# Six banks for the score tiles and two for everything else, in the two attentions with heads of eight columns

## The reference, cut to what matters

```python
latent = x @ Wc_down
q = (latent @ Wq_up).reshape(B, T, 16, 8)
k, v = split(latent @ Wkv_up)              # one k and one v of 8 columns
att = softmax(where(causal, q k^T / sqrt(8), -inf))
x = x + (att @ v).reshape(B, T, 128) @ Wc_proj
```

## Time and profile before

| | us |
|---|---|
| median of three runs | 2706.16 (2706.14 to 2712.98) |
| span of the profiled execution | 2704.96, shown as 2705.0 |
| PE busy | 2422.2 (90%) |
| DVE, ACT, POOL busy | 1665.1, 1493.2, 1428.0 |
| exponentials of `Narrow` (line 1189) | 256, two stages of 128 |

### The profile page before, as it was taken

One profiled execution on the slowest core, in us unless ns is written; L12 is line 12 of the kernel. 1 busy time (PEld: TensorE's weight loads), 2 busy tenths in 40 slices (PEclk: granted clock), 3 DMA queues, 4 the chain that ended last, 5 costly groups with the idle time before them and its releaser, 6 DMA issues. The chain is left out here.

```text
span 2705.0 us, 62888 instructions
## 1 busy us (share of the span) xinstructions
PE 2422.2 (90%) x24633; PEld 1886.2 (70%) x24633; DVE 1665.1 (62%) x4392; ACT 1493.2 (55%) x3193; POOL 1428.0 (53%) x2261
## 2 busy tenths in 40 slices
PE   3999999999997688887999899999999877688887
PEld 3888888888885455556777777777777666455555
DVE  4677777777765567764544466666666522566656
ACT  3666666666653367774444455555555422466664
POOL 4778787787876644433333244444444412665544
PEclk9999999999998789998999999999999989799998
DMA  3691000000000100000000000000000054000000
GB/s 111 215 335 50 2 2 2 2 2 2 2 2 1 36 17 2 2 2 21 2 1 1 3 4 6 5 4 6 5 4 6 7 158 144 17 7 7 4 2 32
DMA packets 23255, 83.14 MB, mean 31 GB/s; under 512 B 4113, under 2 KB 11026, under 8 KB 21938
## 3 DMA queue, kind: packets, MB, share of 16 engines
q1 hardware_dynamic: 19810, 71.90, 8.1%
q0 software_dynamic: 3152, 7.21, 0.8%
HBM read 71.89 MB, written 46.79 MB: 44 GB/s over the span
## 5 line engine op out<-in xcount | busy, mean ns | idle before, releaser
L825 POOL TENSOR_TENSOR XR<-XR,T 128x256 f32<-128x256 f32 x512 | 375.7, 734 | 442.0 <-DVE T L708 411.9
L589 ACT ACTIVATE P<-ps 128x384 f32<-128x384 f32 (+1 forms) x512 | 250.6, 542 | 189.0 <-PE ps L2398 189.0
L2398 PE MATMUL ps<-P,V 128*64 128x256 f32 (+3 forms) x4096 | 332.7, 346 | 2.0 <-ACT P L589 2.0
L1189 ACT ACTIVATE P<-ps 128x768 f32<-128x768 f32 x256 | 207.9, 813 | 148.7 <-PE ps L2398 148.6
L1261 DVE TENSOR_REDUCE qa<-ps 128x2 fp32r<-128x512 f32 x256 | 176.7, 690 | 166.5 <-PE ps L2398 165.2
L2398 PEld LDWEIGHTS ps<-P,V 128*64 128x64 f32 (+1 forms) x4096 | 185.5, 123 | 100.9 <-issue 5.6
L2398 PE MATMUL ps<-mk,identb 128*128 128x256 bf16 (+1 forms) x1024 | 196.9, 295 | 58.9 <-DVE qa L1262 56.6
L719 DVE TENSOR_REDUCE sm<-ps 128x2 f32<-128x512 f32 (+1 forms) x256 | 130.6, 552 | 182.1 <-PE ps L2398 181.3
L1351 POOL TENSOR_SCALAR_AFFINE_SELECT P<-P 128x512 f32<-128x512 f32 x256 | 163.2, 638 | 136.6 <-ACT P L1189 136.2
L836 POOL TENSOR_TENSOR ss<-ss,nhalf 128x16 f32<-128x16 f32 x64 | 187.8, 2935 | 5.3
L2398 PE MATMUL ps<-QH,KH 64*128 64x256 f32 (+1 forms) x1024 | 165.6, 315 | 8.7 <-DVE QL L677 0.6
(11 more groups left out here) (320 smaller groups left out, 7285.5 us busy)
## 6 DMA issues: line engine op xcount, KB each, us to landing
rows_i<-in_zero SPq DMA_DIRECT2D x16, 1208.0 KB, 31.1
rows_o<-in_zero SPq DMA_DIRECT2D x16, 1208.0 KB, 79.6
w<-in_m_w SPq DMA_DIRECT2D x23, 578.0 KB, 4.0
zt<-rows_i SPq DMA_DIRECT2D x23, 128.0 KB, 3.1
rows_o<-yo POOLq DMA_DIRECT2D x23, 128.0 KB, 3.9
stg<-in_t_w SPq DMA_DIRECT2D x11, 256.0 KB, 2.6
XR<-in_x SPq DMA_DIRECT2D x4, 512.0 KB, 7.9
out<-XR SPq DMA_DIRECT2D x8, 256.0 KB, 2.0
```

Of the source, the lines that this page charges most:

```text
L589: e.activation(self.P[at % 6][:, :], K.ps.ap("st", s, g, h)[:, 0:self.w], ACT.Exp, bias=0.0, scale=1.0 if kind == 0 else 0.125).then_inc(K ...
L825: p = po.e.tensor_tensor(x, x, self.T[g % 2][:, par, pr], ALU.add)
L1189: e.activation(self.P[(2 * g + n) % 6][:, :, 0:384], K.ps.ap("st", s, g, n)[:, :, 0:384], ACT.Exp, bias=0.0, scale=self.scale).then_inc(K. ...
L2398: return self.te.matmul(o, l, r, start=start, stop=True, skip_group_check=True)
```

## The change

In class `Narrow` the ring of the scores gets a third pair (banks 4 and 5), which it takes from the ring of single banks. That one keeps banks 6 and 7.

```diff
-    SC, G = (8, 9), (4, 5, 6, 7)
+    SC, G = (8, 9, 10), (6, 7)
```

## The result

The changed kernel takes 2970.59 us (median of 4 runs, 2965.64 to 2972.59) against 2706.15 before: ratio 1.0964, 95% interval 1.0945 to 1.0984. It is slower by 264 us.

A forecast was written before the change was run, and what follows sets the result against it. PE, waiting for DVE's second maximum (line 1262), was taken to bound the kernel. With the lower clock, kind 1's +204 and kind 3's +130, together +332, on 2705.0 gave 3037, given as 3035; range 2850 to 3115 us.

The forecast's parts named there:

- What bounds the kernel: Steady kind 1: PE busiest, 88%, waiting most for DVE's second maximum, line 1262; a loop of about 1.98 us a half-step.
- the third pair: Score ring: masks go ahead of the wait for line 1262, loop 1.98 to 1.66 us; gain at most 77 us.
- Two single banks: Each take waits for the second last one's reader; at full clock +97 us in kind 1, +58 in kind 3.
- The low-clock sum of kind 3: One batch of eight half-steps in kind 3 with the clock at 1.2 GHz throughout: 33.35 us.
- pT's bank: DVE reads pT after both maxima, so takes bound to it start 1.52 us after an exponential's start; pv half-steps 3.14.
- The clock: PE's thin stretches lower it: kind 1 nine tenths low, +204 us; kind 3 half low, +130 us.
- The sum: Whole kernel: 2705.0 + 332 = 3037 us, given as 3035; +155 without the clock.
- Only kind 1 low: Rival: lower clock in kind 1 only, 202 + 58 us, time 2966; chance 0.16.
- The clock stays up: Rival: full clock in both stages, only the waits cost, 2706 + 155 = 2861 us; chance 0.20.
- The gain that was bounded at 77 us: Rival: faster, third pair counts, masks freed from the wait for line 1262, at most 77 us, 2629; chance 0.03.
- the case that I held the likeliest: Clock low in kind 1 and in part of kind 3, 2990 to 3085 us; chance 0.47.
- The page's rule: Cycling through PSUM banks with small PE idle gaps makes the clock swing; by it +332 us, not +155.

The follow-up runs named there:

- alternating pairs: Against the kernel before: still two score pairs and four single banks, but the score ring is (9, 9, 8, 8) in place of (8, 9); 2680.42 us, ratio 0.9897.
- pT first: The changed kernel with DVE's reading of pT put ahead of the maxima of the same tick; 2799.61 us, ratio 1.0345.
- the filler: Kernel with two score pairs and two single banks, plus five useless matmuls into idle bank 4 ahead of each pv; 2938.85 us, 53 less than without them.
- the banks taken by age: Kernel with alternating pairs; in kind 3 the single bank whose last take is oldest, raw's counted 3.5 takes younger; 2662.34 us, ratio 0.9842.

## Why the prediction was right, point by point

- **What bounds the kernel; the third pair.** Shown. The waits of masks for line 1262 are gone and half-steps with no other wait take 1.66, the number forecast. With two single banks the pair is worth 20 us; nearly the same effect without a third pair gives 26 (alternating pairs). The bound on the gain was too low: in kind 3 the masks are 0.43 and not 0.32, which makes it 91 us and not 77.
- **Two single banks.** Shown, by releaser and by size: 16 half-steps forecast, 15 of them within 0.12 of the measured ones, and P3 of kind 1 (4.0) within 0.14 of what it takes where the clock stays low (4.14). The price of a pair of transposes, 0.22, is right, though the scaling that the prediction gives for it comes to 0.20. The low-clock sum of kind 3, 33.35, was never reached, so it isn't tested.
- **pT's bank.** Shown by pT first: the four Q half-steps of kind 1 fall from 4.2 (low clock; 3.1 by the sum at the full clock) to between 1.66 and 2.22 in the batches with the clock up.
- **The clock.** Shown for kind 1 by the filler: more work, 76 us less. The forecast for kind 1, 30.5 a batch, is what was measured (30.44 to 31.4). In kind 3 I took half of the time at each level, 28.5 a batch; the 13 batches between 2535.79 and 2878.42 average 26.4, and PEclk 0.86 from the first to the last exponential means the lower level in 28% of the time. Most falls came where they were forecast, in P2 or Q2, but most rises came in Q3, four half-steps ahead of the next Q1 where I had put it, and three batches had no fall at all.
- **The sum.** +332 forecast, +264 measured. Mis-sized are two terms. In kind 3, +8.6 a batch was +6.1 (26.4 less the 20.2 of the same batches before), and in both kinds I multiplied by 15.1 batches where only 13 have all of their prep. In the last two batches no raw, zT or lt is left, PE waits less and the clock is up: in kind 1 the 13 batches give +174 of the +177, in kind 3 +80 of the +85. With 13 batches and 6.1 the same working gives 175 + 79 = 254; the other ten lie between the stages (4) and in their first and last batches. As an estimate, the loss is some 155 us of waits (105 in kind 1, and 24.07 less 20.2 in 13 batches of kind 3) and some 105 of clock.
- **The rivals.** "Only kind 1 low", 2966, lies nearest to the time, but not for its reason: kind 3 wasn't up throughout (PEclk 0.86) and kind 1 cost less than 202. "The clock stays up" is excluded by the windows. The gain that was bounded at 77 us came to 26 when it was had without the loss. The measured 2971 lies in the whole range, which is 265 us wide, but below the 2990 to 3085 of the case that I held the likeliest: its mechanism was right and its size wasn't.
- **The page's rule.** The Trainium skill, "TensorE: Matmul & The Clock Gate", section "A second HAM failure mode: psum-queue depth-cycling", tells of a kernel that cycles through PSUM banks and whose short PE idle times between groups of matmuls make the clock swing between its levels. This trace agrees: PE was never idle for more than 1.6 us in kind 1, PEclk went to 0.54, and the clock went up and down once in most batches of both stages.

## What to carry to other kernels

Before banks are taken from a ring, write down for each tile who reads it and what stands ahead of that reader on its engine. A ring of n banks makes each take wait for the reader of the n-th last tile, and a small tile that is read late (pT, raw) costs the in-order PE more than a large one that is read early. A pair of buffers whose two users free them at different times can be swapped between the users, instead of adding a third. And a PE that stays 84% busy while its matmuls per microsecond fall from 11.1 to 6.1 hasn't become the bottleneck: look at the granted clock first.

## What the runs showed of the hardware

The clock fell in a stage (kind 1) that never left PE idle for more than 1.6 us at a time, and it stayed low for most of 380 us at a PE busy share of 84%. Nor did every unbroken stretch of work raise it soon. From the changed kernel (PE busy and count, PEclk, DMA), first the start of kind 3, then a rise in kind 1:

```profile
2502.50:2512.80 10.30, 10.30 (x50) 0.51 0.05 14
...
1232.70:1236.30 3.60, 3.60 (x30) 0.50 0.02 5
1236.30:1239.70 3.40, 1.71 (x17) 1.00 0.00 0
```

The first row is 10.3 us of transposes, masks and scores on end, and the clock rose only after them, at 2512.88. In the second, 3.6 us on end with a pv among them were followed by a rise at once. So the prediction's reading of the earlier trace rows, that the clock rose only after work without a break, holds for these rows too, but such work alone doesn't say when the clock rises; which matmuls count for it, the runs don't say.

Open too is what makes Q2 of kind 3 0.7 us longer in seven batches, the third to the ninth, before and with alternating pairs. In the kernel before, the exponential starts 0.76 after the end of the last score matmul there and 0.1 elsewhere. In each of the seven, POOL begins a gather (line 1336) 0.04 after the scores end:

```profile
2445.71 0.22 PE L2398 MATMUL ps<-kz,qT 32*128 32x128 f32 x2
...
2445.98 0.96 POOL L1336 DMA_INDIRECT back<-rows_o,place  x1 [0.30 <-issue]
...
2446.69 0.81 ACT L1189 ACTIVATE P<-ps 128x768 f32<-128x768 f32 x1 [1.12 <-PE ps L2398]
```

The later batches have no gather, and with the banks taken by age it starts 0.6 us after the exponential. With the change in kind 1 only, kind 3 runs the code of the kernel before, and yet in six such batches Q2 takes 3.03 and Q3 2.82 in place of 2.14: a lengthening of the same size at another place. So the bank order alone doesn't decide it. That the gather is the cause isn't shown; no run was made for it.
